# The first feed-forward rows handled inside the last attention turns

## The chip, the cores and the metric

The kernel runs on one core of one Trainium2 chip. The metric is the device time of one execution in microseconds (us); shorter is better. Where a profile is read, its own execution has a time and a span of its own, and both are named.

## The reference

A one-layer language model on 64 sequences of 128 tokens, model width 512. Everything is float32.

```
h = table[x] + lora_A.T[x] @ lora_B.T                       # embedding
h = h + attention(layernorm(h))                             # 16 heads, causal, low-rank q and kv
h = h + ffn(layernorm(h))

def ffn(x2):                                                # x2: 8192 x 512
    shared = x2 @ sw1.T * square(relu(x2 @ swg.T)) @ sw2.T  # hidden 256
    xl = x2 @ Wdown.T                                       # 128 wide
    probas = sigmoid(x2 @ Wg.T)                             # 16 experts
    top 8 of (probas + biases) per token; p = probas there, scaled to sum 2.5
    acc = sum over experts e of w[:, e] * (xl @ rw1[e].T * square(relu(xl @ rwg[e].T)) @ rw2[e].T)
    return shared + acc @ Wup.T
```

## The kernel before, in words

Each matrix product is made of three passes over a value split in a high and a low part (`split_matmul`): high times high, high times low, low times high. ScalarE (ACT) usually copies the high part out, VectorE (DVE) subtracts it to get the low part. "Splitting a piece" of the weights is such a pair of copies.

The program has two phases, each an engine-by-engine program of its own in a block. A block ends in a barrier that all engines must reach, and the next one starts behind it. Buffers in SBUF are allotted per phase, so nothing of the second phase is in place before the first one is over.

The **attention phase** treats 16 groups of 4 sequences (512 tokens) in a software pipeline. It is written out as turns n = -2 to 16 of 16 steps each. In turn n the scores, exponentials and head outputs of group n are made, while the front of group n+2 (`FRONT`: the gather's part `art`, the embedding rows `h`, the transposes `xt` of the normalised rows, the down projection `wd`) and the output projection `out` of group n-1 run between them. Tables (`MIDWAY`, `END`) say which of these parts stands in which step, and `has_part` says in which turns it exists: the front is absent in turns 14, 15 and 16, which have no group left to open. In turn 16 only the last head outputs of group 15 and its output projection are left. PE is TensorE. The SP queue issues all plain transfers in order: it stores the embedding rows `h`, loads them again into `res`, DVE adds the projection (`add_out`), and SP stores the result to the DRAM array `h2`. At its end SP waits for all these stores (`stored`).

The **expert phase** (`ffn_phase`) treats 16 groups of 512 rows of `h2`, group 0 by straight code, the rest in a loop. A group's front is: load `x`, statistics and inverse deviation on DVE, normalise on ACT, transposes on PE, high part `fxT_hi` and low part `fxT_lo`, the gate's product (`route_logits`), the down projection (`to_latent`), routing on DVE, and the two shared hidden halves. For groups 1 to 15 it is done between the expert products of the group before. For group 0 it stands alone at the phase's start, together with the constants (`gate`, identity) and the first 8 of 16 weight pieces of 128x1024, which come through staging buffers and are split on ACT and DVE. The routing weights leave as rows `wT` to the DRAM array `w_rows` and come back spread over all partitions (`w_all`, one transfer of 256 KB per expert); DVE multiplies by them in `weigh`. The remaining 8 pieces are loaded and split during group 0.

## Time and profile before

| | before |
|---|---|
| time, median of 3 runs (lowest, highest) | 2556.54 us (2556.44, 2558.4) |
| the profiled execution: its own time | 2557.69 us |
| the profiled execution: span | 2555.9 us |
| PE busy | 2434.7 us, 95% of the span |
| ACT busy | 1820.4 us, 71% |
| DVE busy | 1709.8 us, 67% |
| POOL (GpSimd) busy | 1131.6 us, 44% |
| mean granted TensorE clock | 0.987 of full |

The times of this document's traces are in microseconds from the start of the span. L401 is line 401 of the profiled kernel. Busy shares are means over the whole span; what one stretch waits for must be read in that stretch. The matmuls are pipelined, so the durations of two in a row overlap; what one costs is the distance of two starts.

### The profile page before, as it was taken

What the parts mean: (1) busy time and instruction counts of PE and PEld (TensorE: products, weight loads), DVE (VectorE), ACT (ScalarE), POOL (GpSimd) and SP (SyncE); (2) the same over time, 40 slices, a digit from 0 to 9 for tenths busy, and PEclk for the clock granted to TensorE, in tenths of its full rate; (3) what the DMA queues carried; (4) which work ended last, traced back from release to release, by engine and by line L of the source; (5) the groups of instructions that cost most, each with busy time, mean ns of one, the idle gap of its engine ahead of it and who ended that gap; (6) DMA issues with size and microseconds to landing.
All of it is one profiled execution on the core that took longest, in us unless ns stands there. A gap on an engine that the chain in (4) does not pass through costs nothing.

```text
span 2555.9 us, 47538 instructions
## 1 busy us (share of the span) xinstructions
PE 2434.7 (95%) x13632; PEld 1872.0 (73%) x13632; DVE 1709.8 (67%) x3614; ACT 1820.4 (71%) x4597; POOL 1131.6 (44%) x1275
## 2 busy tenths in 40 slices
PE   3899999999999996899999999999999999999999
PEld 2666666666777664678888888888888888878887
DVE  6777777777777763667567557657657657657655
ACT  2777777777777783677678668669668668668766
POOL 3444444444444331245445446436436445445444
PEclk8999999999999998899999999999999999999999
DMA  3222222222222112423213213212212221321321
GB/s 106 68 68 68 80 70 69 72 76 81 79 79 69 51 34 100 128 71 108 87 37 111 87 42 105 87 54 92 89 66 76 95 83 53 96 85 49 99 73 60
DMA packets 99830, 198.24 MB, mean 78 GB/s; under 512 B 10928, under 2 KB 10928, under 8 KB 99568
## 3 DMA queue, kind: packets, MB, share of 16 engines
q1 hardware_dynamic: 94576, 179.29, 21.2%
q0 software_dynamic: 5120, 17.31, 2.8%
q8 instruction: 67, 1.10, 0.2%
q14 instruction: 67, 0.55, 0.1%
HBM read 145.66 MB, written 50.86 MB: 77 GB/s over the span
## 4 chain that ended last, share of the span: by engine, by line
issue 30%; POOL 25%; PE 2%; DVE 1%; ACT 1%; POOLq 1%; DMA 0%; SPq 0%; DVEq 0%; ACTq 0%
POOL t_lo L1194 24%; POOL sh_lo L1194 2%; POOLq L1192 1%; DVE ps_u L1563 0%; DVE f_lo L1588 0%; ACT x L1357 0%; DMA x<-h 0%; DVE t L1570 0%; ACT t_hi L1412 0%; PE ps_g L1209 0%; PE fwork L1209 0%; PE ps_u L1211 0%; PE ps_u L1209 0%; PE ps_g L1211 0%; PE ps_g L1210 0%
## 5 line engine op out<-in xcount | busy, mean ns | idle before, releaser
L1194 POOL TENSOR_TENSOR t_lo<-t,t_hi 128x512 fp32r<-128x512 f32 x512 | 665.0, 1299 | 423.7 <-ACT t_hi L1412 423.6
L401 POOL TENSOR_TENSOR probs<-probs,inv 128x512 f32<-128x512 f32 x256 | 266.4, 1042 | 470.6 <-DVE inv L819 469.7
L1563 DVE TENSOR_TENSOR ps_u<-ps_u,square 128x512 f32<-128x512 f32 x512 | 357.2, 698 | 155.8 <-ACT square L1399 151.6
L1412 ACT ACTIVATE t_hi<-t 128x512 fp32r<-128x512 f32 x512 | 320.4, 626 | 121.0 <-PE ps_y L1211 68.3
L1570 DVE TENSOR_TENSOR t<-ps_u,w_all 128x512 f32<-128x512 f32 x512 | 354.1, 692 | 64.5 <-DVE ps_u L1563 22.4
L1395 ACT ACTIVATE square<-ps_g 128x512 f32<-128x512 f32 x544 | 319.7, 588 | 91.4 <-PE ps_g L1211 89.3
L637 ACT ACTIVATE probs<-ps_s,nmax 128x128 f32<-128x128 f32 x1024 | 364.1, 383 | 18.4 <-DVE nmax L813 17.3
L1399 ACT ACTIVATE square<-square 128x512 f32<-128x512 f32 x544 | 344.1, 633 | 17.3
L637 ACT ACTIVATION_READ_ACCUMULATOR probs<-ps_s,nmax 128x1 f32 x1024 | 228.7, 223 | 0.0
L1209 PE MATMUL ps_y<-t_hi,f_hi 128*128 128x512 f32 x512 | 210.2, 410 | 12.2 <-POOL t_lo L1194 12.0
L1194 POOL TENSOR_TENSOR sh_lo<-t,sh_hi 128x512 fp32r<-128x512 f32 x32 | 41.7, 1302 | 401.1 <-ACT sh_hi L1412 401.1
L1209 PE MATMUL ps_u<-xl_hi,f_hi 128*128 128x512 f32 x512 | 201.6, 394 | 5.3 <-DVE t L1570 5.3
L1209 PE MATMUL ps_g<-xl_hi,f_hi 128*128 128x512 f32 x512 | 201.1, 393 | 0.0
L1211 PE MATMUL ps_u<-xl_hi,f_lo 128*128 128x512 f32 x512 | 201.0, 393 | 0.0
L1210 PE MATMUL ps_y<-t_lo,f_hi 128*128 128x512 f32 x512 | 200.9, 392 | 0.0
L1211 PE MATMUL ps_y<-t_hi,f_lo 128*128 128x512 f32 x512 | 200.7, 392 | 0.0
L1211 PE MATMUL ps_g<-xl_hi,f_lo 128*128 128x512 f32 x512 | 200.6, 392 | 0.0
L1210 PE MATMUL ps_u<-xl_lo,f_hi 128*128 128x512 f32 x512 | 200.6, 392 | 0.0
L1210 PE MATMUL ps_g<-xl_lo,f_hi 128*128 128x512 f32 x512 | 200.3, 391 | 0.0
L644 ACT ACTIVATE pT<-ps_t 128x512 f32<-128x512 f32 x256 | 158.4, 619 | 29.7 <-PE ps_t L535 27.9
L813 DVE TENSOR_REDUCE nmax<-ps_s 128x8 f32<-128x1024 f32 x128 | 156.0, 1219 | 26.4 <-PE ps_s L526 25.7
L535 PE MATMUL ps_t<-ident,probs 128*128 128x128 f32 x1024 | 164.6, 283 | 9.2 <-ACT pT L644 7.7
(198 smaller groups left out, 5380.8 us busy)
## 6 DMA issues: line engine op xcount, KB each, us to landing
w_all<-w_rows SPq DMA_DIRECT2D x256, 256.0 KB, 3.2
h<-h SPq DMA_DIRECT2D x64, 256.0 KB, 2.1
res<-h SPq DMA_DIRECT2D x64, 256.0 KB, 2.8
h<-res SPq DMA_DIRECT2D x64, 256.0 KB, 2.0
x<-h SPq DMA_DIRECT2D x16, 1024.0 KB, 5.7
fres<-h SPq DMA_DIRECT2D x16, 1024.0 KB, 7.5
out<-fres SPq DMA_DIRECT2D x64, 256.0 KB, 2.1
fres<-in_w_ffn SPq DMA_DIRECT2D x14, 512.0 KB, 3.6
```

What stands on the lines that cost most here:

```text
L401: pool.tensor_tensor(probs[:, s % RING, :, :], probs[:, s % RING, :, :], inv[:, s % RING, :].rearrange("p (h o) -> p h o", o=1).to_broadca ...
L535: mm = pe.transpose(ps_t[:, j * P:(j + 1) * P], probs[:, s % RING, j, :], ident[:, :])
L637: e = act.activation(probs[:, s % RING, j, :], ps_s[:, b, x, i, y, :], ACT.Exp, bias=nmax[:, b, x, i, y:y + 1], accum_out=total[:, s % RIN ...
L1194: pool.tensor_tensor(lo, t[:, t_slot(j), :], hi.bitcast(F32), ALU.subtract).then_inc(t_lo_done, 1)
L1209: pe.matmul(o, a_hi, b_hi, start=first, stop=False)
L1210: pe.matmul(o, a_hi, b_lo, start=False, stop=False)
L1211: return pe.matmul(o, a_lo, b_hi, start=False, stop=last)
L1395: act.activation(square[:, j % 2, :], ps_g[:, j % 2, :], ACT.Relu).then_inc(relu_done, 1)
L1399: act.activation(square[:, j % 2, :], square[:, j % 2, :], ACT.Square).then_inc(square_done, 1)
L1412: act.activation(dst, t[:, t_slot(j), :], ACT.Copy).then_inc(t_hi_done, 1)
L1563: dve.tensor_tensor(dst, product, square[:, j % 2, :], ALU.mult).then_inc(t1_done, 1)
L1570: dve.tensor_tensor(t[:, t_slot(j), :], ps_u[:, u_bank(j), :], w_all[:, e % 2, :], ALU.mult).then_inc(t_done, 1)
```

## The change: what it does

- Buffers that both phases use are allotted once, outside both: the attention's `h` becomes `rows` (the experts' `x`), its `xn` becomes `keep` (the experts' staging and residual buffer), its `res` also holds `w_all` and `wT`, and `xT_hi`, `xT_lo`, the identity and the gate's buffers are shared.
- Turn 14 of the attention gets the part `xt` again, with statistics and normalisation, for a "group 16": the first 512 rows of `h2`, which turn 1 finished. SP loads them at the start of turn 14, with gate and biases; DVE prepares the gate.
- At the start of turn 15 SP loads weight pieces 0 to 3 into `keep` and `rows`.
- In turn 16 the output projection waits for each quarter (chunk) of the head outputs by itself, and for tiles 0 and 1 the first two of four chunks are issued in steps 0 and 1, ahead of the last head outputs.
- SP no longer waits for the last stores at the end of the attention; the experts wait for them where they reuse `res`.
- The experts' group 0 begins with `route_logits`. Pieces 4 to 7 are loaded after the barrier, pieces 8 and 9 after the first two spreads, group 1's rows ahead of the routing rows. Splits, routing and the shared halves stand in another order.

```diff
     if part == "out":
         return not any(is_turn(n, k) for k in (-2, -1, 0))
+    if part == "xt":
+        return not any(is_turn(n, k) for k in (GROUPS - 1, GROUPS))
...
         nw = sb("nw", [P, 5, 2 * TILES], F32)
-        xn = sb("xn", [P, TILES, D], F32)
-        xT_hi = sb("xT_hi", [P, DC, TOK], F32R)
-        xT_lo = sb("xT_lo", [P, DC, TOK], F32R)
+        xn, xT_hi, xT_lo = shared.keep, shared.xT_hi, shared.xT_lo
...
+            def load_first_rows():
+                sp.dma_start(shared.gate_raw[:, :, :], w_gate).then_inc(shared.small_loaded, 16)
+                sp.dma_start(shared.bias[:, :], biases).then_inc(shared.small_loaded, 16)
+                for t in range(TILES):
+                    wait_alone(sp, res_kept[t], 16 * GROUPS, sp_passed)
+                    wait_alone(sp, stored[t], 16, sp_passed)
+                wait_alone(sp, xn_done, TILES * GROUPS, sp_passed)
+                sp.dma_start(h[:, :, :], h2[0:TOK, :].rearrange("(t p) d -> p t d", p=P)).then_inc(rows_loaded, 16)
+
+            def load_first_pieces():
+                for t in (2, 3):
+                    bank, before = place(GROUPS - 2, "xt", t)
+                    wait_alone(sp, work_free[bank], DRAINS * (before + 1), sp_passed)
+                for i in range(4):
+                    sp.dma_start(piece_rows((shared.keep, shared.rows)[i // 2], i % 2),
+                                 w_ffn[:, i * PIECE:(i + 1) * PIECE]).then_inc(shared.piece_loaded[i], 16)
+
             def turn(n, side):
+                if is_turn(n, GROUPS - 2):
+                    load_first_rows()
+                if is_turn(n, GROUPS - 1):
+                    load_first_pieces()
...
-            for t in range(TILES):
-                sp.wait_ge(stored[t], 16 * GROUPS)
...
-                    if step == RSTD_AT and has_part(n, "h", 0):
+                    if step == RSTD_AT and has_part(n, "xt", 0):
...
-            def out_proj(n, side, t):
-                pe.wait_ge(oT_lo_done, DC * n)
-                for m in range(DC):
+            def out_proj(n, side, t, chunks=range(DC)):
+                if not is_turn(n, GROUPS):
+                    pe.wait_ge(oT_lo_done, DC * n)
+                for m in chunks:
+                    if is_turn(n, GROUPS):
+                        pe.wait_ge(oT_lo_done, DC * (n - 1) + m + 1)
...
+                        elif part == "out" and is_turn(n, GROUPS) and i < 2:
+                            mm = out_proj(n, side, i, range(2, DC))
...
+                    if is_turn(n, GROUPS) and step < 2:
+                        empty(pe, n, "out", step)
+                        out_proj(n, side, step, range(2))
...
-                drained(dve, n, "h", t)
+                if has_part(n, "h", t):
+                    drained(dve, n, "h", t)
+                else:
+                    dve.wait_ge(rows_loaded, 16)
...
-                front, rows = has_part(n, "h", 0), has_part(n, "ct", 0)
+                front, rows = has_part(n, "xt", 0), has_part(n, "ct", 0)
...
-                        if step == SPLIT_AT and not is_turn(n, GROUPS - 3):
+                        if step == SPLIT_AT and is_turn(n, GROUPS - 2):
+                            prepare_gate()
+                        elif step == SPLIT_AT and not is_turn(n, GROUPS - 3):
...
-FIRST_USES = 8
+FIRST_USES = 4
...
+        ident, gate, bias = shared.ident, shared.gate, shared.bias
+        x, res = shared.rows, shared.keep
...
+        w_all, wT = shared.res[:, 0:2, :], shared.res[0:EXPERTS, 2, :]
...
-            if i in (2, 3):
-                return (square, t)[i - 2][:, 0:2, :].rearrange("p b k -> p (b k)")
-            return res[:, :, :].rearrange("p t d -> p (t d)")[:, (i % 2) * PIECE:(i % 2 + 1) * PIECE]
+            if i in (4, 5):
+                return t[:, 2 * (i - 4):2 * (i - 3), :].rearrange("p b k -> p (b k)")
+            return piece_rows(x if i in (2, 3) else res, i % 2)
...
-                return 0
+                return -V_LOGITS // 2
...
-            sp.dma_start(gate_raw[:, :, :], w_gate).then_inc(small_loaded, 16)
-            sp.dma_start(bias[:, :], biases).then_inc(small_loaded, 16)
...
+                if before is None:
+                    wait_alone(sp, piece_lo, 4, sp_passed)
+                else:
...
-            load_x(0, None)
-            for i in range(EARLY_PIECES + 2):
+            for i in range(4, EARLY_PIECES):
                 load_piece(i)
+            load_x(1, None)
             store_rows(0)
+            for i in range(TILES):
+                wait_alone(sp, shared.stored[i], 16 * GROUPS, sp_passed)
             spread(0, 0)
             spread(0, 1)
+            for i in range(EARLY_PIECES, EARLY_PIECES + 2):
+                load_piece(i)
             def group(g, more):
-                if more:
+                first = isinstance(g, int) and g == 0
+                if more and not first:
                     load_x(g + 1, g)
-                first = isinstance(g, int) and g == 0
...
-            pool.memset(fident[:, :], 0.0).then_inc(f_ident, 1)
-            pool.wait_ge(f_ident, 1)
-            pool.affine_select(out=fident[:, :], in_=fident[:, :], compare_op=ALU.not_equal, fill=1.0,
-                               base=0, pattern=[[-1, P]], channel_multiplier=1).then_inc(f_ident, 1)
...
+                if isinstance(g, int) and g == 0:
+                    act.wait_ge(shared.stored[2], 16 * GROUPS)
                 full(act, half, k)
...
+            first = front_half(0)
             split(0)
-            for i in range(TILES):
-                normalise(0, i)
             split(1)
-            for i in range(TILES):
-                x_hi(0, 0, i)
+            logits_copy(0, first)
             split(2)
             split(3)
-            logits_copy(0, 0)
-            latent_hi(0, 0)
+            latent_hi(0, first)
+            logits_back(0, first)
+            sigmoid(0)
             split(4)
-            logits_back(0, 0)
-            sigmoid(0)
             split(5)
+            weights_copy(0, first)
             squares(0, 0)
             squares_end(0, 0)
             split(6)
+            hidden_hi(0, 0)
             squares(0, 1)
             squares_end(0, 1)
             split(7)
-            weights_copy(0, 0)
-            hidden_hi(0, 0)
             group(0, True)
...
-            dve.memset(gate[:, :, :].bitcast(F32), 0.0).then_inc(f_zeroed, 1)
-            dve.wait_ge(f_zeroed, 1)
-            dve.wait_ge(small_loaded, 32)
-            dve.tensor_copy(gate[:, :, 0:EXPERTS], gate_raw[:, :, :]).then_inc(small_step, 1)
-            dve.wait_ge(small_step, 1)
-            dve.tensor_tensor(gate[:, :, EXPERTS:2 * EXPERTS], gate_raw[:, :, :],
-                              gate[:, :, 0:EXPERTS].bitcast(F32), ALU.subtract).then_inc(small_step, 1)
-            for part in range(TILES + 1):
-                x_moments_of(0, part)
-            x_seed(0)
-            for k in range(3):
-                x_rstd(0, k)
-            x_shift(0)
-            split(0)
-            split(1)
-            for i in range(TILES):
-                x_lo(0, 0, i)
-            split(2)
-            split(3)
-            latent_lo(0, 0)
+            first = front_half(0)
+            for i in range(4):
+                split(i)
+            latent_lo(0, first)
+            routing(0, first)
             split(4)
-            routing(0, 0)
             split(5)
+            dve.wait_ge(piece_lo, 6)
             linear(0, 0)
             split(6)
             linear(0, 1)
```

Three places show how the instructions move. In these rows a bracket names the semaphores that an instruction waits for.

PE at the end of the attention (turn 16), before: `ps_t` are the transposes of the last probabilities, `ps_o` the head outputs, `work` with `oT_hi` the output projection.

```order
L535 MATMUL ps_t<-ident,probs 128x128 [waits pT_done,probs_done]
L535 MATMUL ps_t<-ident,probs 128x128 x3
L547 MATMUL ps_o<-pT,v 32x128 [waits pT_done,oT_lo_done]
...
L434 MATMUL work<-w_hi,oT_hi 128x512 [waits oT_lo_done,work_free0]
L435 MATMUL work<-w_lo,oT_hi 128x512
L436 MATMUL work<-w_hi,oT_lo 128x512
```

The same place now; the first row is the transposes of step 0.

```order
L591 MATMUL ps_t<-ident,probs 128x128 x3
L487 MATMUL work<-w_hi,oT_hi 128x512 [waits oT_lo_done,work_free0]
L488 MATMUL work<-w_lo,oT_hi 128x512
L489 MATMUL work<-w_hi,oT_lo 128x512
L487 MATMUL work<-w_hi,oT_hi 128x512 [waits oT_lo_done]
L488 MATMUL work<-w_lo,oT_hi 128x512
L489 MATMUL work<-w_hi,oT_lo 128x512
L591 MATMUL ps_t<-ident,probs 128x128 [waits pT_done,probs_done]
L591 MATMUL ps_t<-ident,probs 128x128 x3
```

Six projection matmuls of tile 0 stand between two sets of transposes; six of tile 1 stand behind the second set in the same way, so 12 of the 48 moved ahead of the head outputs.

DVE behind the barrier, before: `fstats` to `shift` are the first rows' statistics, `f_lo` a weight piece's low part, `fxT_lo` the transposed rows' low part, `xl_lo` the latent's.

```order
L1476 UNCONDITIONAL_BRANCH [waits barrier_Pool_Activation_PE_DVE_SP_release]
L1621 MEMSET gate 128x512
L1624 CAST gate<-gate_raw 128x4x16 [waits small_loaded,f_zeroed]
L1626 TENSOR_TENSOR gate<-gate_raw,gate 128x4x16 [waits small_step]
L1481 BN_STATS fstats<-x 128x6 [waits x_loaded] x4
...
L90 TENSOR_SCALAR shift<-fnw 128x4 [waits shift_done]
L1588 TENSOR_TENSOR f_lo<-fres,f_hi 128x1024 [waits piece_hi] x2
L1504 TENSOR_TENSOR fxT_lo<-fwork,fxT_hi 128x4x128 [waits fxT_hi_done] x4
L1588 TENSOR_TENSOR f_lo<-square,f_hi 128x1024 [waits piece_hi]
L1588 TENSOR_TENSOR f_lo<-t,f_hi 128x1024 [waits piece_hi]
L1511 TENSOR_TENSOR xl_lo<-fwork,xl_hi 128x512 [waits xl_hi_done]
```

DVE behind the barrier now:

```order
L1560 UNCONDITIONAL_BRANCH [waits barrier_Pool_Activation_PE_DVE_SP_release]
L1672 TENSOR_TENSOR f_lo<-keep,f_hi 128x1024 [waits piece_hi] x2
L1672 TENSOR_TENSOR f_lo<-rows,f_hi 128x1024 [waits piece_hi] x2
L1595 TENSOR_TENSOR xl_lo<-fwork,xl_hi 128x512 [waits xl_hi_done]
L1612 TENSOR_TENSOR route<-weights 128x64 [waits fwork_free0]
```

Gate, statistics and `fxT_lo` are gone from here; they stand in turn 14.

SP from turn 14 to turn 15 now; before, the rows of L376, L377, L382 and L389 did not exist. L407 is the store of a finished tile, L415 the reload of one.

```order
L415 DMA res<-h 128x512 [waits stored3,res_kept3]
L376 DMA gate_raw<-in_w_gate 128x64
L377 DMA bias<-in_biases 128x16
L382 DMA rows<-h 128x4x512 [waits res_kept0,stored0,res_kept1,stored1,res_kept2,stored2,res_kept3,stored3,xn_done]
L407 DMA h<-res 128x512 [waits work_free0]
...
L389 DMA keep<-in_w_ffn 128x1024 [waits work_free1,work_free0]
L389 DMA keep<-in_w_ffn 128x1024
L389 DMA rows<-in_w_ffn 128x1024 x2
L407 DMA h<-res 128x512 [waits work_free0]
```

The new loads stand between the last reload of one turn and the first store of the next.

## Rows read from the trace of the kernel before

**Rows 1.** Windows: busy us of PE, PEld, DVE, ACT, POOL; TensorE clock, DMA share, GB/s

```profile
860.20:916.80 56.60, 54.99 (x429) 39.36 (x429) 36.59 (x85) 44.91 (x170) 18.96 (x28) 1.00 0.12 39
916.80:965.20 48.40, 46.94 (x364) 31.90 (x366) 26.73 (x48) 41.32 (x164) 16.59 (x16) 1.00 0.14 45
1006.80:1032.30 25.50, 3.89 (x17) 3.17 (x17) 11.52 (x37) 8.07 (x12) 0.50 (x2) 0.57 0.50 177
1060.90:1103.00 42.10, 38.12 (x143) 28.07 (x144) 39.28 (x68) 35.31 (x58) 20.67 (x16) 0.92 0.48 150
```

**Rows 2.** Waits, 975 to 1070 us: who waited for whom, total us, times, longest

```profile
PE fwork L1223 <- ACT x L1357: 17.8, 1, 17.8
```

**Rows 3.** Timeline of the SP queue: start, length, line, transfer

```profile
880.86 0.34 SPq L360 DMA_DIRECT2D res<-h  x1
916.81 6.74 SPq L352 DMA_DIRECT2D h<-res  x2
998.55 8.70 SPq L352 DMA_DIRECT2D h<-res  x4
1053.71 0.35 SPq L1141 DMA_DIRECT2D w_rows<-wT  x1
1057.25 0.81 SPq L1149 DMA_DIRECT2D w_all<-w_rows  x2
```

**Rows 4.** Timeline of PE: a transposed tile in attention, then turn 16

```profile
815.79 0.60 PE L465 MATMUL work<-ident,xn 128*128 128x128 f32 x4
816.22 0.60 PE L535 MATMUL ps_t<-ident,probs 128*128 128x128 f32 x4
...
986.62 1.09 PE L535 MATMUL ps_t<-ident,probs 128*128 128x128 f32 x4 [1.25 <-ACT pT L644]
989.51 1.93 PE L547 MATMUL ps_o<-pT,v 128*32 128x128 f32 x32
992.98 0.76 PE L434 MATMUL work<-w_hi,oT_hi 128*128 128x512 f32 x1 [1.53 <-DVE oT_lo L824]
...
996.52 0.41 PE L436 MATMUL work<-w_hi,oT_lo 128*128 128x512 f32 x1
1005.59 0.40 PE L436 MATMUL work<-w_hi,oT_lo 128*128 128x512 f32 x1
```

**Rows 5.** Timeline around the barrier: POOL and DVE

```profile
1009.39 0.20 POOL L1186 MEMSET fident<- 128x128 f32 x1 [22.07 <-POOLq L187]
1009.57 0.48 DVE L1621 MEMSET gate<- 128x512 f32 x1 [2.75 <-SPq L187]
```

**Rows 6.** Timeline of PE in the experts' opening

```profile
1032.29 0.76 PE L1233 MATMUL fwork<-fxT_hi,gate 128*128 128x512 f32 x1 [1.61 <-DVE fxT_lo L1504]
1037.53 0.40 PE L1210 MATMUL fwork<-fxT_lo,f_hi 128*128 128x512 f32 x1
1061.62 0.79 PE L1209 MATMUL ps_u<-xl_hi,f_hi 128*128 128x512 f32 x1 [5.06 <-DVE t L1570]
```

**Rows 7.** Timeline of ACT in the opening

```profile
1041.30 1.28 ACT L1383 ACT_TABLE_LOAD   x1
1042.76 1.04 ACT L1420 ACTIVATE f_hi<-fres 128x1024 fp32r<-128x1024 f32 x1
1051.77 0.59 ACT L1388 ACTIVATE wT<-fwork 16x512 f32<-16x512 f32 x1 [0.24 <-PE fwork L1257]
```

**Rows 8.** Timeline of DVE in the opening

```profile
1045.61 0.22 DVE L1547 SCALAR_TENSOR_TENSOR weights<-route,wsum 128x64 f32<-128x64 f32 x1
1047.48 1.22 DVE L1588 TENSOR_TENSOR f_lo<-fres,f_hi 128x1024 fp32r<-128x1024 f32 x1
1060.87 0.69 DVE L1570 TENSOR_TENSOR t<-ps_u,w_all 128x512 f32<-128x512 f32 x1 [6.12 <-DMA w_all<-w_rows]
```

**Rows 9.** DMA issues of the page: queue, form, count, KB, median us to landing

```profile
h<-res SPq DMA_DIRECT2D x64, 256.0 KB, 2.0
t<-in_w_ffn SPq DMA_DIRECT2D x1, 512.0 KB, 8.8
```

More of the change, by code:

```diff
@@ L12 @@
 from contextlib import ExitStack
+from dataclasses import dataclass
 F32 = mybir.dt.float32
@@ L180, in place, with attention_phase, piece_rows, attention @@
     return k % 2, before + k // 2
-def attention_phase(nc, table, tok, lora_b, w_attn, ln, h2):
+@dataclass
+class Shared:
+    rows: object
+    keep: object
+    res: object
+    xT_hi: object
+    xT_lo: object
+    ident: object
+    gate_raw: object
+    gate: object
+    bias: object
+    piece_loaded: list
+    small_loaded: object
+    gate_zeroed: object
+    gate_step: object
+    stored: list
+operands_of_attention = []
+def attention_phase(nc, *operands):
+    operands_of_attention.append(operands)
+def piece_rows(buffer, i):
+    return buffer[:, :, :].rearrange("p t d -> p (t d)")[:, i * PIECE:(i + 1) * PIECE]
+def attention(nc, shared, w_ffn, w_gate, biases, table, tok, lora_b, w_attn, ln, h2):
     with ExitStack() as ctx:
@@ L195, in sem @@
             return ctx.enter_context(nc.semaphore(name))
-        ident = sb("ident", [P, P], F32)
+        ident = shared.ident
         ident_r = sb("ident_r", [P, P], F32R)
@@ L215, in attention_phase @@
         arT = sb("arT", [3 * RANK, TOK], F32R)
-        h = sb("h", [P, TILES, D], F32)
-        res = sb("res", [P, TILES, D], F32)
+        h, res = shared.rows, shared.res
         stats = sb("stats", [P, TILES, 6], F32)
@@ L289, in attention_phase @@
         res_loaded = [sem(f"res_loaded{t}") for t in range(TILES)]
-        stored = [sem(f"stored{t}") for t in range(TILES)]
+        stored = shared.stored
+        rows_loaded = sem("rows_loaded")
         dve_passed = sem("dve_passed")
@@ L957, in sb, with sem, experts @@
             return ctx.enter_context(nc.sbuf_tensor(name, shape, dt))
+        def sem(name):
+            return ctx.enter_context(nc.semaphore(name))
+        shared = Shared(
+            rows=sb("rows", [P, TILES, D], F32), keep=sb("keep", [P, TILES, D], F32),
+            res=sb("res", [P, TILES, D], F32), xT_hi=sb("xT_hi", [P, DC, TOK], F32R),
+            xT_lo=sb("xT_lo", [P, DC, TOK], F32R), ident=sb("ident", [P, P], F32),
+            gate_raw=sb("gate_raw", [P, DC, EXPERTS], F32), gate=sb("gate", [P, DC, P], F32R),
+            bias=sb("bias", [P, EXPERTS], F32), piece_loaded=[sem(f"piece{i}") for i in range(PIECES)],
+            small_loaded=sem("small_loaded"), gate_zeroed=sem("gate_zeroed"), gate_step=sem("gate_step"),
+            stored=[sem(f"stored{t}") for t in range(TILES)])
+        attention(nc, shared, w_ffn, w_gate, biases, *operands_of_attention.pop())
+        experts(nc, shared, h2, w_ffn, w_rows, out)
+def experts(nc, shared, h2, w_ffn, w_rows, out):
+    with ExitStack() as ctx:
+        def sb(name, shape, dt):
+            return ctx.enter_context(nc.sbuf_tensor(name, shape, dt))
         def pb(name, shape, dt):
@@ L976, in ffn_phase @@
         shift = sb("shift", [P, TILES], F32)
-        xT_hi = sb("fxT_hi", [P, DC, TOK], F32R)
-        xT_lo = sb("fxT_lo", [P, DC, TOK], F32R)
+        xT_hi, xT_lo = shared.xT_hi, shared.xT_lo
         xl_hi = sb("xl_hi", [P, TOK], F32R)
@@ L992, in ffn_phase @@
         weights = sb("weights", [P, TILES, 2 * EXPERTS], F32)
-        wT = sb("wT", [EXPERTS, TOK], F32)
-        w_all = sb("w_all", [P, 2, TOK], F32)
+        w_all, wT = shared.res[:, 0:2, :], shared.res[0:EXPERTS, 2, :]
         ps_g = pb("ps_g", [P, 2, TOK], F32)
@@ L999, in ffn_phase @@
         work = pb("fwork", [P, 2, 512], F32)
-        s_piece = [sem(f"piece{i}") for i in range(PIECES)]
+        s_piece = shared.piece_loaded
         piece_hi = sem("piece_hi")
         piece_lo = sem("piece_lo")
-        small_loaded = sem("small_loaded")
-        f_zeroed = sem("f_zeroed")
-        f_ident = sem("f_ident")
-        small_step = sem("small_step")
         x_loaded = sem("x_loaded")
@@ L1116, in load_x @@
             def load_x(g, before):
-                if before is not None:
+                if before is None:
+                    wait_alone(sp, piece_lo, 4, sp_passed)
+                else:
                     wait_drained(front_half(before), V_XT + 2)
@@ L1223, in x_turn @@
                     mm = pe.transpose(work[:, i % 2, m * P:(m + 1) * P], x[:, i, m * P:(m + 1) * P],
-                                      fident[:, :])
+                                      ident[:, :])
                 mm.then_inc(work_full[i % 2], 1)
             def route_logits(g, half):
-                drained(pe, half, V_XT + 2)
-                drained(pe, half, V_XT + 3)
+                if not (isinstance(g, int) and g == 0):
+                    drained(pe, half, V_XT + 2)
+                    drained(pe, half, V_XT + 3)
                 empty(pe, half, V_LOGITS)
@@ L1325, in group @@
                     logits_turn(g + 1, half)
-                    shared(g + 1, 0)
-                    shared(g + 1, 1)
+                    shared_half(g + 1, 0)
+                    shared_half(g + 1, 1)
                     weights_turn(g + 1, half)
```

71 lines of the change are left out of this document (36 added, 35 removed).

## The prediction

> **What bounds the kernel now.** I first read the busy shares over the span, which say that PE is the bound, and then asked in windows where it is not. In the attention's turns PE is busy nearly all the time: 54.99 of 56.60 us from step 8 of turn 13 to step 8 of turn 14, and 46.94 of 48.40 us one turn later [rows 1]. Between the phases it is not: from 1006.8 to 1032.3 us it does 3.89 us of work in 25.50 us [rows 1]. The waits name the cause: 17.8 us of PE waiting for ACT's normalised first rows [rows 2]. The timeline tells the rest. POOL leaves the barrier at 1009.39 us [rows 5]; call that R. PE's first product, the gate's, starts at 1032.29 [rows 6], that is R+22.9. Then the routing rows make their round trip through DRAM: `wT` is copied at 1051.77 [rows 7], stored by SP at 1053.71, spread from 1057.25 [rows 3], and DVE's first `weigh` starts at 1060.87 after 6.12 us of idleness [rows 8]. PE stands 5.06 us until 1061.62 [rows 6]. So the opening, from R to the first `weigh`, takes 51.5 us. Behind it DVE, with 39.28 of 42.10 us busy [rows 1], and not PE, limits group 0 while pieces 8 to 15 are split. So I measure the opening at DVE's first `weigh`.
>
> **Term 1, turn 14 (+1.9 us).** Four tiles of four transposes are added. PE takes 0.43 us from the start of such a tile to what follows it [rows 4], 4 x 0.43 = 1.7 us. PE is the bound there, so it is on the path; I add 0.2 for small waits. DVE gets the statistics, normalisation, four low parts and the gate, ACT four copies of high parts. DVE is busy 26.73 of 48.40 us in the later window and 36.59 in the earlier one [rows 1], so this has room and is costed at nothing; without that room it would show as waits of PE for `xT_lo`. Lower bound 1.7. Upper bound: the two windows differ by 56.60 - 48.40 = 8.2 us, which holds this work and the down projection too.
> The loads of turn 14 and 15 are put at nothing. SP issues nothing from 880.86+0.34 to 916.81 us [rows 3], and at about 882 all that they wait for is done; the four pieces go out at about 948, and the next store, of turn 15, is far off. Their price if late: turn 14's first stores would stand behind them.
>
> **Term 2, the attention's tail (-5.0 us).** Before, 48 projection matmuls run from 992.98 to 1005.99 [rows 4]. The clock is low at first (starts 0.43 us apart, full 0.23), and full from 996.52 on. Now 12 matmuls lie in the gaps where PE waits for ACT's copies, 1.25 us before 986.62 [rows 4]: six at full clock take 6 x 0.23 = 1.4 us. Three more (tile 0's third chunk) fill the 1.53 us wait for the last low part. 33 are left. At full clock they take 33 x 0.23 = 7.6 instead of 13.0 us, gain 5.4; with eight at the low clock, as before, 1.6 less, gain 3.8. If the denser work keeps the clock up, the head outputs of 1.93 us [rows 4] shrink by some 0.8 too, gain 6.2. Between 3.8 and 6.2 I take 5.0. Other bound: the six-matmul packets run at the low clock, 2.6 us each in gaps of 1.25; that delays the transposes behind them by 1.3 twice, gain 1.2.
> The Trainium skill ("TensorE: Matmul & The Clock Gate", Part 1 on the clock gate) says that PE is granted 2.4 GHz while it has been busy and 1.2 GHz after idleness. The trace agrees that the level falls in this sparse stretch. By that rule the packets would rather keep the clock up, gain 6.2 and a total 1.2 us lower than mine.
>
> **Term 3, no wait for the last stores (-1.7 us).** The last store is issued at 998.55+8.70 = 1007.25 us [rows 3]. Issued some 0.33 earlier, it lands 2.0 us later [rows 9], at about 1008.95; the barrier opens 0.45 later. Now it should open 0.45 after the issue, at 1007.7. Bounds: 0 (if the barrier itself takes that long) and 2.1.
>
> **Term 4, the opening (-29.6 us).** Gate, statistics, normalising, transposes and `fxT_lo` are gone from behind the barrier, and pieces 0 to 3 lie ready. From the new R on:
> - PE starts at R+0.2 at the low clock (it idled at the barrier): 8 gate matmuls x 0.43 = 3.4, to R+3.6. Before, the clock rose 5.2 us after 1032.29 (row at 1037.53 [rows 6]). So of the 12 down-projection matmuls four are slow: 1.7 + 8 x 0.23 = 3.5, to R+7.1.
> - ACT splits take 1.0 each [rows 7], DVE's 1.22 [rows 8]. Two splits, the logits copy at R+3.7, two more splits: piece 2 is done on DVE at R+6.5, piece 3 at R+7.7. PE's first shared half (24 matmuls x 0.23 = 5.6) goes from R+7.6 to R+13.2.
> - Routing: logits back at R+8.0, table load 1.28 [rows 7] to R+9.3; from a table load's end, 1042.58 [rows 7], to `weights`, 1045.83 [rows 8], it took 3.3: R+12.6. Weights turned behind the first half: R+13.7. `wT` copied, 0.59 [rows 7]: R+14.3. From 1053.71 to 1057.25 and on to 1060.87 the round trip takes 3.5 + 3.6 [rows 3, 8]: `w_all` is there at R+21.5. SP gets to the store at once, since its waits on pieces and rows ahead of it end by R+7.7.
> - Meanwhile PE's second half ends at R+19.3; DVE's product, split 7 and the next product (0.7 + 1.2 + 0.7) end at R+21.9. That is when `weigh` starts.
> 51.5 - 21.9 = 29.6. Bounds: PE at full clock throughout, 0.9 better; PE at the low clock through all 68 matmuls (0.2 us more for each of the 56 that I counted fast), 11 worse.
>
> **Term 5, behind it (-0.5 us).** PE's stretch of low clock after the 5.06 us wait disappears, worth 15 matmuls x 0.2 = 3.1, but DVE limits there. It waited only a little. From 0 to 3.1 I take 0.5. Pieces 8 and 9 are requested only after the spreads, at R+18 and R+21.2, and are used after R+25.
>
> **Sum.** 1.9 - 5.0 - 1.7 - 29.6 - 0.5 = -34.9 us. The profiled execution took 2557.69 us (span 2555.9); it becomes 2522.8. It lies 1.15 above the median of 2556.54, which becomes 2521.6.
>
> **The rivals.**
> - *The clock stays up* in turn 16 and early in the opening: 1.2 better there, 0.9 here and 1.5 of term 5: 2518. For it: the gaps are filled. Against it: PE must idle at the barrier. Chance 0.13, all gains beyond 2518 included.
> - *A transfer takes the place of the wait.* Pieces 4 and 5 go into `t` only behind the barrier; such a load took 8.8 us [rows 9] when many ran together, R+9.5, just when ACT wants it. Or piece 9, which waits on DVE's split 7, holds up SP's next spreads. Both have cover of 0 to 5 us. If it is used up, `weigh` slips by 3 to 7 us: 2525 to 2529. Chance 0.15.
> - *Code is late at the barrier.* Behind it each engine jumps to new code. Before, PE had 17.8 us of waiting to hide that [rows 2]; now nothing hides it. DVE began 0.2 us after POOL [rows 5], which speaks against it. The nearest row for a small transfer is the 3.5 us of the routing rows [rows 3]: with one or two on the path, 2525 to 2528. Chance 0.07. The Trainium skill ("Runtime: NRT & Kernel Launch", Instruction fetch mechanics) says that a taken branch to a page that is not at hand stalls until it is fetched. It names no price for it.
> - *The change doesn't do what it says*: the splits on ACT and DVE keep PE waiting as long as the rows did. They are 4 x 1.22 us in the stretch, so this would need each to wait for a transfer. Gain under 20, above 2537. Chance 0.04.
> - *Slower.* One mechanism: SP's queue. The load of the first rows waits in order for the last normalisation of turn 13; if it isn't free by 916.81, stores and reloads of turn 14 stand behind it and so does `add_out`. It has 35.6 us of room [rows 3], and must be late by that and 34.9 us more before the kernel is slower: over 2562. Chance 0.02, no change 0.01.
>
> **How the numbers follow.** The forecast, 2518.5 to 2525, has 0.58. With the clock rival and the two late ones a range of 2515 to 2529 holds what is wanted; bounds of term 1 and term 4 beyond it are left out with the last two rivals. About 0.2% (5 us) is what a measurement of this kernel tells from no change. Faster 0.97, same 0.01, slower 0.02.
>
> **What the changed profile would show.** Turn 14 about 2 us longer, without PE waits over 1 us for `xT_lo`. Last projection matmul 5 us earlier relative to the head outputs. Barrier under 1.2 us behind the last `add_out`. The gate's first matmul 0.2 us behind it, the first `weigh` 22 us behind it, with no PE wait of 5 us. Wrong it would be if PE, ACT or DVE stood several us right behind the barrier, if the store of `wT` came late on SP, or if the loss in turn 14 were above 4 us.

## The result, and the profile after

The changed kernel takes 2518.76 us (median; 2518.29 to 2520.05), the one before 2556.49 in the same comparison. The ratio is 0.9851, 95% interval [0.984, 0.9863]: 1.5% faster. The profiled execution took 2518.29 us, its span is 2516.5; that is 39.4 less than the span before. In what follows R is the first instruction behind the barrier: POOL at 1009.39 before [rows 5], SP at 1007.80 after.

The page of the changed kernel, and its windows (columns as in [rows 1]) over the part of turn 14 that got longer and over the opening:

```profile
span 2516.5 us, 47561 instructions
PE 2421.6 (96%) x13632; PEld 1866.1 (74%) x13632; DVE 1707.6 (68%) x3604; ACT 1814.8 (72%) x4593; POOL 1134.3 (45%) x1285
...
937.20:971.70 34.50, 32.19 (x255) 21.11 (x255) 20.18 (x38) 30.43 (x123) 11.39 (x11) 0.95 0.25 85
1006.10:1029.40 23.30, 21.32 (x95) 16.75 (x95) 16.49 (x34) 17.07 (x25) 3.12 (x2) 1.00 0.62 200
```

The second window is the gain. PE was busy for 3.89 of 25.50 us at the phase's start [rows 1]; now it is for 21.32 of 23.30, at full clock. The first shows what was paid: the clock is 0.95 where it was 1.00.

The SP queue, the counterpart of [rows 3]:

```profile
1000.12 7.30 SPq L407 DMA_DIRECT2D h<-res  x4
1007.80 0.84 SPq L1223 DMA_DIRECT2D t<-in_w_ffn  x2
...
1020.64 0.34 SPq L1228 DMA_DIRECT2D w_rows<-res  x1
1022.30 0.82 SPq L1236 DMA_DIRECT2D res<-w_rows  x2
```

The barrier opens 0.4 us after the last store is issued (1000.12 + 7.30 = 1007.42), no longer when it has landed. The routing rows are stored 12.8 us behind it, where it took 44.3, and spread 1.66 later (3.54 before).

PE in turn 16 and in the opening, the counterpart of [rows 4, 6]:

```profile
991.33 0.63 PE L591 MATMUL ps_t<-ident,probs 128*128 128x128 f32 x4 [1.16 <-ACT pT L705]
...
993.22 0.63 PE L591 MATMUL ps_t<-ident,probs 128*128 128x128 f32 x4
...
995.61 1.18 PE L603 MATMUL ps_o<-pT,v 128*32 128x128 f32 x32
998.24 0.50 PE L487 MATMUL work<-w_hi,oT_hi 128*128 128x512 f32 x1 [0.55 <-DVE oT_lo L888]
...
1005.78 0.39 PE L489 MATMUL work<-w_hi,oT_lo 128*128 128x512 f32 x1
1007.86 0.47 PE L1320 MATMUL fwork<-xT_hi,gate 128*128 128x512 f32 x1 [1.69 <-PEq L223]
```

The wait ahead of the second tile of `ps_t` is gone, since six matmuls fill it. The head outputs take 1.18 us instead of 1.93. The gate's first matmul starts 0.06 us behind R and is 0.47 us long instead of 0.76: full clock.

DVE and ACT up to the first `weigh`, the counterpart of [rows 7, 8]:

```profile
1018.39 0.23 DVE L1631 SCALAR_TENSOR_TENSOR weights<-route,wsum 128x64 f32<-128x64 f32 x1
1019.96 0.59 ACT L1475 ACTIVATE res<-fwork 16x512 f32<-16x512 f32 x1 [2.42 <-PE fwork L1344]
...
1027.50 0.70 DVE L1647 TENSOR_TENSOR ps_u<-ps_u,square 128x512 f32<-128x512 f32 x1
1028.23 0.69 DVE L1654 TENSOR_TENSOR t<-ps_u,res 128x512 f32<-128x512 f32 x1
```

`weigh` (`t<-ps_u,res`) follows the product ahead of it without a wait. It is no longer the round trip through DRAM that ends last there, but PE's shared halves and DVE's products.

### The profile page after: what moved, and what is told of

The parts are those of the page before. It is cut to its first block, busy times and chain, and to the rows that moved or that the text cites. A ratio compares the mean times of both kernels' runs of the same rounds, so it can differ in the third digit from the quotient of the medians.

```text
span 2516.5 us, 47561 instructions
## 1 busy us (share of the span) xinstructions
PE 2421.6 (96%) x13632; PEld 1866.1 (74%) x13632; DVE 1707.6 (68%) x3604; ACT 1814.8 (72%) x4593; POOL 1134.3 (45%) x1285
## 4 chain that ended last, share of the span: by engine, by line
issue 30%; POOL 26%; PE 2%; DVE 1%; ACT 1%; POOLq 1%; DVEq 0%; ACTq 0%
POOL t_lo L1280 24%; POOL sh_lo L1280 2%; POOLq L1278 1%; DVE ps_u L1647 0%; DVE f_lo L1672 0%; DVE t L1654 0%; ACT t_hi L1499 0%; PE fwork L1295 0%; PE ps_g L1295 0%; ACT square L1482 0%; PE ps_g L1297 0%; PE ps_g L1296 0%; PE ps_u L1297 0%; PE ps_u L1295 0%; PE ps_u L1296 0%
## 5 line engine op out<-in xcount | busy, mean ns | idle before, releaser
L1654 DVE TENSOR_TENSOR t<-ps_u,res 128x512 f32<-128x512 f32 x512 | 354.0, 691 | 55.5 <-DVE ps_u L1647 22.4
```

Source lines behind the costliest of these rows:

```text
L1654: dve.tensor_tensor(t[:, t_slot(j), :], ps_u[:, u_bank(j), :], w_all[:, e % 2, :], ALU.mult).then_inc(t_done, 1)
```

## The experiments

Each changes the changed kernel, except where said. Times of places come from the traces.

**Turn 16: the projection late again.**

```diff
-                        elif part == "out" and is_turn(n, GROUPS) and i < 2:
-                            mm = out_proj(n, side, i, range(2, DC))
...
-                    if is_turn(n, GROUPS) and step < 2:
-                        empty(pe, n, "out", step)
-                        out_proj(n, side, step, range(2))
```

> The changed kernel with one part undone: in turn 16 the output projection of all four tiles stands behind the last low part again, 48 matmuls in a row, as in the kernel before. Everything else is as changed. In the traces the stretch from the transposes of step 0 of turn 16 to the end of the last projection matmul took 21.25 us before and 14.84 us in the changed kernel. Theory 1 (15 matmuls moved into gaps, and with the gaps filled the clock stays at 2.4 GHz, so that the head outputs and the 33 left are fast too): this kernel takes some 21.2 us there, 6.4 more than the changed one, and its granted clock falls before the projection; time about 2525.1 us. Rival (only the matmuls moved count, 15 x 0.23 us, the clock stands high for another reason): 3.5 us more, 2522.2 us, with head outputs of 1.2 us and matmuls 0.23 us apart from the start.

2525.67 us, ratio 0.9878 [0.9861, 0.9894], thus 6.9 us slower than the changed kernel by the ratios, whose intervals just touch. But the profiled execution, the shortest of four, has a span of 2520.8, only 4.3 more, and a stretch of 19.14 us. So I took a second profile of this kernel:

> The same kernel as e_late_proj, profiled once more. Its profiled execution had a span of 2520.8 us and a mean granted clock of 0.995; its three other executions 2523.8 to 2525.8 at 0.993. Theory 1 (in these the clock fell in the thin stretch of turn 16 and stayed low into the 48 matmuls, as in the kernel before, where 13.01 us passed from the first of them to the end of the last): an execution with a span of 2523 to 2526 shows 12.5 to 13.5 us there, against 11.41 in the first profile. Rival (the low stretches are elsewhere, at the start of the kernel or in turn 14): a span of 2523 to 2526 with 11.4 us there and the first store of turn 1 later than 157. If the span is 2521 again, nothing is told.

The second span is 2523.6. PE's timeline in turn 16, first of the one execution, then of the other:

```profile
995.62 1.93 PE L600 MATMUL ps_o<-pT,v 128*32 128x128 f32 x32
999.09 0.47 PE L487 MATMUL work<-w_hi,oT_hi 128*128 128x512 f32 x1 [1.54 <-DVE oT_lo L880]
...
1010.10 0.40 PE L489 MATMUL work<-w_hi,oT_lo 128*128 128x512 f32 x1
```

```profile
991.08 0.63 PE L588 MATMUL ps_t<-ident,probs 128*128 128x128 f32 x4 [1.17 <-ACT pT L697]
...
995.19 1.94 PE L600 MATMUL ps_o<-pT,v 128*32 128x128 f32 x32
998.66 0.77 PE L487 MATMUL work<-w_hi,oT_hi 128*128 128x512 f32 x1 [1.53 <-DVE oT_lo L880]
...
1012.49 0.40 PE L489 MATMUL work<-w_hi,oT_lo 128*128 128x512 f32 x1
```

In both the head outputs run at 1.2 GHz (1.93 us). In the first the 48 matmuls start at full clock (0.47) and take 11.41 us, in the second at half (0.77) and take 14.23; the stretch is 21.81 us. One program, one place, 2.8 us apart by when the clock comes back; I had expected 12.5 to 13.5 us for the 48, so the half clock lasted longer than that. Theory 1 holds with 7.0 us in the second execution (14.84 to 21.81). In the first it is 4.3 us, with the clock low in the transposes and heads but not in the 48. The rival's 3.5 is only the part of the matmuls that were moved.

**Turn 16: one tile instead of two.** `i < 2` and `step < 2` above become `i < 1` and `step < 1`.

> The changed kernel with half of the early projection: in turn 16 only tile 0's first two chunks (6 matmuls) and its third stand in the gaps ahead; tile 1 is projected in one piece at the end as before. With all of it late the stretch from the transposes of step 0 of turn 16 to the end of the last projection matmul took 19.14 us, the eight head outputs in a row took 1.93 us (low clock), and the matmuls behind them stood 0.23 us apart; in the changed kernel it took 14.84 us and the head outputs 1.18. Theory 1 (one filled gap is enough to keep the clock): the head outputs take 1.2 us and the stretch is 6 x 0.233 = 1.4 us longer than in the changed kernel, 16.2 us. Rival (the clock falls in the second gap, which is empty again): the head outputs take 1.9 us and the stretch 17.0 to 18.5 us.

```profile
994.54 0.63 PE L591 MATMUL ps_t<-ident,probs 128*128 128x128 f32 x4
995.94 0.63 PE L591 MATMUL ps_t<-ident,probs 128*128 128x128 f32 x4 [0.78 <-ACT pT L705]
996.50 1.18 PE L603 MATMUL ps_o<-pT,v 128*32 128x128 f32 x32
```

The heads take 1.18 us although the second gap is open: in this execution one filled gap kept the clock. The stretch is 15.81 us (992.65 to 1008.46), 0.97 more than with two tiles, not 1.4: the second packet of six is longer than its gap and had put the heads off by 0.43 (from the first `ps_t` to the heads 3.85 here, 4.28 there). The time, 2521.58 us, ratio 0.9859 [0.9842, 0.9875], doesn't tell it from the changed kernel.

**The wait for the last stores, put back.**

```diff
             for n in range(-2, GROUPS + 1):
                 turn(n, n % 2)
+            for t in range(TILES):
+                sp.wait_ge(stored[t], 16 * GROUPS)
```

> The changed kernel with one part undone: SP waits again, at the end of the attention, for the last stores to land, so the barrier opens later. Theory 1: the opening keeps its length and only slides: from the end of the last add_out to the first issue behind the barrier 2.5 to 2.8 us instead of 0.8, and the whole time is 1.75 us longer, about 2520.5. Rival (the clock): PE idles 1.69 us at the barrier in the changed kernel and its first gate matmul still has the full clock; with 3.4 us of idleness the clock falls to 1.2 GHz, the first matmuls stand 0.43 us apart, and 8 to 20 of them at 0.2 us more put another 1.6 to 4 us on top: 2522 to 2524.

2522.7 us, 0.9866 [0.9849, 0.9882]; span 3.2 over the changed kernel's. The intervals of the two ratios overlap, so the reading rests on the trace. The opening in its timeline:

```profile
1009.55 0.76 PE L1320 MATMUL fwork<-xT_hi,gate 128*128 128x512 f32 x1 [3.46 <-PEq L223]
1010.11 0.63 PE L1320 MATMUL fwork<-xT_lo,gate 128*128 128x512 f32 x1
...
1015.22 0.39 PE L1297 MATMUL fwork<-xT_hi,f_lo 128*128 128x512 f32 x1
...
1031.98 0.69 DVE L1654 TENSOR_TENSOR t<-ps_u,res 128x512 f32<-128x512 f32 x1
```

The rival is right. The barrier is 1.8 us later (R at 1009.51), and behind 3.46 us of idleness PE runs at half clock until 1015.2: from R to `weigh` 22.47 us instead of 20.43. Dropping the wait is worth 1.8 us by itself and 2.0 by the clock up to `weigh`; 0.5 of it is made good again behind.

**The first weight pieces behind the barrier.** `load_first_pieces()` is not called; the experts' SP begins with `for i in range(EARLY_PIECES)` instead of `range(4, EARLY_PIECES)`.

> The changed kernel with one part undone: weight pieces 0 to 3 are not loaded in turn 15 but are SP's first issues behind the barrier, ahead of pieces 4 and 5. Theory 1 (the pieces' load is a part of its own of the gain): such a load took 8.8 us in the kernel before when several ran together, and 3.6 alone, so that the first split starts 4 to 7 us behind the barrier instead of at once. The gate's matmuls and the routing go on, but the down projection, the first shared half and all products behind it slip by that: the first product with square, 13.99 us behind the first issue in the changed kernel, comes at 18 to 21, and the time is 4 to 7 us longer, 2523 to 2526. PE idles there and falls to the low clock as well, which could put 1 to 3 us more on it. Rival (the round trip of the routing rows covers it): the weights of the experts were spread by 24 us behind the barrier at the latest, so up to 2 us of slip cost nothing, and the time is under 2 us longer.

```profile
1011.98 1.06 ACT L1505 ACTIVATE f_hi<-keep 128x1024 fp32r<-128x1024 f32 x1 [14.25 <-DMA keep<-in_w_ffn]
...
1014.35 0.80 PE L1293 MATMUL fwork<-xT_hi,f_hi 128*128 128x512 f32 x1 [4.17 <-DVE f_lo L1670]
```

The first split starts 3.9 us behind R (1008.07), PE stands 4.17 us and comes back at half clock. From R to `weigh` it takes 26.39 us, 5.96 more: the down projection starts 3.9 us later behind R, and its 12 matmuls take 4.77 us from first to last start instead of 2.67. The time is 2525.68 us, 0.9878 [0.9862, 0.9895]. Theory 1 holds; the round trip covers nothing.

**Turn 14: the inversion first.** The row in question, in the changed kernel's timeline of DVE, POOL, PE and ACT:

```profile
940.97 0.61 ACT L660 ACTIVATE xT_hi<-work 128x512 fp32r<-128x512 f32 x1
941.68 0.69 DVE L813 TENSOR_TENSOR xT_lo<-work,xT_hi 128x512 fp32r<-128x512 f32 x1 [2.13 <-ACT xT_hi L660]
942.29 0.17 DVE L883 RECIPROCAL inv<-total 128x4 f32<-128x4 f32 x1
942.53 1.04 POOL L454 TENSOR_TENSOR probs<-probs,inv 128x512 f32<-128x512 f32 x1 [3.04 <-DVE inv L883]
943.63 0.82 PE L591 MATMUL ps_t<-ident,probs 128*128 128x128 f32 x4 [1.96 <-POOL probs L454]
945.23 2.08 PE L582 MATMUL ps_s<-k_diag,qT 64*128 64x256 f32 x8
```

DVE stands 2.13 us at `xT_lo`, whose `xT_hi` is behind four exponentials on ACT. The reciprocal behind it has its totals already: with the edit below it runs before this wait. POOL and then PE wait for it, and the clock falls to half (2.08 us for what takes 1.14).

```diff
-                    if step in INVERT_FIRST and has_slot(n, step - INV_LAG):
+                    early = step in INVERT_FIRST or (is_turn(n, GROUPS - 2) and step == SPLIT_AT)
+                    if early and has_slot(n, step - INV_LAG):
```

> The changed kernel with one thing more: in turn 14 DVE inverts the totals of step 13 ahead of the other work of step 14, thus ahead of the low part of transposed tile 3, which waits for ACT. Theory 1 (head of the line): the low part of tile 3 blocks DVE's queue for 2.1 us, the reciprocal behind it is late, POOL's scaling of the probabilities behind that, and PE waits 1.96 us, upon which the clock falls to half for 3 us. With the reciprocal ahead the wait of PE is under 0.5 us, the clock stays up, and 2.5 to 3.1 us come back in turn 14: about 2515.5 us. Rival (it is POOL or ACT that is late in turn 14, by the added copies of xT_hi): the reciprocal comes earlier, PE's wait stays above 1.5 us and the time within 0.5 us of 2518.3. A third way: the gate's three operations behind it, 2.2 us in all, delay the next two reciprocals, so that a second wait appears and only 1 to 2 us come back.

```profile
939.41 0.18 DVE L883 RECIPROCAL inv<-total 128x4 f32<-128x4 f32 x1 [0.40 <-ACT probs L698]
942.85 0.69 DVE L813 TENSOR_TENSOR xT_lo<-work,xT_hi 128x512 fp32r<-128x512 f32 x1 [2.13 <-ACT xT_hi L660]
943.38 0.63 PE L591 MATMUL ps_t<-ident,probs 128*128 128x128 f32 x4 [1.08 <-ACT pT L705]
944.37 1.13 PE L582 MATMUL ps_s<-k_diag,qT 64*128 64x256 f32 x8
```

DVE waits as long as before, but nothing that is ready stands behind it. From turn 13's first store to turn 15's it takes 107.40 us instead of 109.81, the clock stays, and the time is 2516.65 us, 0.9841 [0.9825, 0.9857]. This interval overlaps that of the changed kernel, so the gain of the time is not shown by itself; that of the place is, since the changed kernel's profile and the five of the experiments above, which leave turn 14 alone, have 109.51 to 109.98 us there. A wait of 1.08 us is left, now for ACT.

**And the gate in turn 15.** `prepare_gate()` moves to step 8 of turn 15.

> The changed kernel with the inversion of turn 14 put ahead of the other work of step 14, as in the run before this one that did that alone, and with the gate's memset, cast and low part moved from DVE's step 14 of turn 14 to step 8 of turn 15. With the inversion alone, turn 14 was 2.4 us shorter (107.40 us from the first store of turn 13 to that of turn 15, against 109.81) and PE had one wait of 1.08 us left there, for ACT's pT. Theory 1: the gate's operations (1.25 us of DVE, and the gaps between them) still hold up the reciprocals of steps 14 and 15 in turn 14; with them gone another 0.3 to 0.7 us come back, about 2516. Rival: what is left is the four tiles of transposes themselves (1.75 us) and ACT's copy in front of pT, and the gate costs nothing: 107.4 us again and 2516.5.

From turn 13's first store to turn 15's it takes 107.38 us, and the time is 2517.71 us, 0.9848 [0.9832, 0.9865]: the rival's case; the gate costs nothing.

**Placement: the kernel before with the experts' buffers elsewhere.** The groups of the loop got shorter, and the attention's turns longer, without a changed instruction. In the kernel before `x`, `fres`, `w_all`, `wT`, 2 KB unused, `fxT_hi`, `fxT_lo`, `fident` and the gate's buffers are allotted ahead of `f_hi`.

> The kernel before, with nothing changed but the order in which the buffers of the feed-forward phase are allotted, so that every one of them (x, residual, w_all, wT, both halves of xT, the weights and all that follows) lies at the address that it has in the changed kernel. The attention's buffers stay where they were. The changed kernel took 93.49 us for a group of the feed-forward loop, the kernel before 93.83, with the same instructions. Theory 1 (the place of the buffers in SBUF sets how many nanoseconds a matmul takes): this kernel takes 93.5 us per group, 13 x 0.34 and a little at the ends, 5 to 6 us less in all: about 2551. Rival (it is something else that differs, such as where the instructions lie in memory, or one execution against another): 93.8 us per group and the time of the kernel before, within 1 us of 2556.5.

The first output store of groups 1 and 14, of before, of this kernel and of the changed one:

```profile
1249.47 0.36 SPq L1131 DMA_DIRECT2D out<-fres  x1
...
2469.32 0.36 SPq L1131 DMA_DIRECT2D out<-fres  x1
```

```profile
1247.76 1.47 SPq L1132 DMA_DIRECT2D out<-fres  x2
...
2463.48 5.55 SPq L1132 DMA_DIRECT2D out<-fres  x4
```

```profile
1215.62 5.51 SPq L1218 DMA_DIRECT2D out<-keep  x4
...
2430.89 5.53 SPq L1218 DMA_DIRECT2D out<-keep  x4
```

A thirteenth of the distance is 93.83, 93.52 and 93.48 us. (The profiles of the changed kernel and of its variants without pads lie between 93.48 and 93.56.) The place thus makes 4.1 of the 4.6 us that the 13 groups lost, and the median falls too: 2552.74 us, 0.9983 [0.9974, 0.9993]. Outside these groups it shows as well. From the first `weigh`, which here still waits for the round trip, to the end of the span it takes 1489.06 us instead of 1495.03:

```profile
1060.04 0.69 DVE L1571 TENSOR_TENSOR t<-ps_u,w_all 128x512 f32<-128x512 f32 x1 [6.06 <-DMA w_all<-w_rows]
```

The attention, whose buffers are not moved here, keeps its 58.59 us a turn (58.78 in the changed kernel; a twelfth of the distance from turn 1's to turn 13's first store).

**Placement: pads in the changed kernel.**

```diff
         ident = shared.ident
+        sb("pad", [P, 472], F32)
...
+        sb("fpad", [P, 152], F32)
         f_hi = sb("f_hi", [P, W_FFN], F32R)
```

> The changed kernel with two unused buffers and nothing else: 1888 bytes per partition ahead of the attention's own buffers, 608 ahead of the experts' own. The kernel before, with the experts' buffers placed as in the changed one, took 93.52 us per group of the loop instead of 93.83, so the place matters there. Theory 1 (what counts is how the two operands of a matmul lie to each other within 2 KB, or their alignment): the pad gives the attention's weights the distance from the transposed rows that they had in the kernel before, so that a turn takes 58.57 us again instead of 58.75; and it changes the groups' 93.49 by 0.1 us or more. Rival (what counts is in which region of SBUF a buffer lies, thousands of bytes away): 58.75 and 93.49 stay within 0.03.

58.56 us a turn, and 93.63 a group: both moved. The turn did so clearly (without a pad it is 58.77 to 58.81 in eight profiles), the group by 0.07 us beyond the range above. The median is 2517.13 us, 0.9844 [0.9827, 0.986]. The profiled execution, at 2521.29 us, was the longest of four; its start was late (first store of turn 1 at 159.97, not 156.53), with the down projections ahead of it at half clock for longer. With 32 bytes in either place (8 elements):

> The changed kernel with 32 unused bytes per partition ahead of the attention's own buffers and 32 ahead of the experts' own. This puts the attention's weights, which begin 32 bytes past a multiple of 64, onto a multiple of 64 like the transposed rows, and takes the experts' weights off one. Theory 1 (alignment to 64 bytes counts): a turn falls from 58.78 to about 58.56 us as with the pad of 1888 bytes, and a group gets longer than 93.50. Rival (the distance within some hundreds or thousands of bytes counts, which 32 bytes hardly change): 58.75 to 58.80 us a turn and 93.48 to 93.55 us a group.

58.69 us a turn and 93.60 a group, less than half of the way in the turns; 2518.56 us, 0.9847 [0.9832, 0.9862]. So alignment to 64 bytes is not the whole of it, and neither theory holds alone. Where it sits can be read from the mean distance between the starts of neighbouring matmuls, worked out from the timelines (48 of each over three turns; other turns give means up to 1 ns away). The first two rows are the down projection's 256-column matmuls, the third the output projection's of 512 columns:

```
                          before   after   pad 1888   pad 32
w_hi,xT_hi -> w_lo,xT_hi   131.9   137.1   130.4      135.4 ns
w_lo,xT_hi -> w_hi,xT_lo   115.2   119.4   114.8      118.3 ns
w_hi,oT_hi -> w_lo,oT_hi   255.0   255.8   255.6      256.0 ns
```

Those that read `xT`, which was moved relative to the attention's weights, change by 4 to 7 ns between before, the changed kernel and the pad of 1888 bytes; those that read `oT`, which was moved together with the weights, don't. Forty-eight such distances a turn at 4.2 ns make the 0.2 us.

**The gains together**: inversion first, gate in turn 15, the pad of 1888 bytes.

> Three things put together on the changed kernel: the inversion of turn 14 ahead of step 14's other work, the gate's preparation in turn 15, and an unused buffer of 1888 bytes per partition ahead of the attention's own buffers (none ahead of the experts'). Theory 1 (the gains add, because they come at different places): turn 13's first store to turn 15's 107.38 us less two turns' 0.22, so 106.9; 58.56 us per turn instead of 58.78, 16 x 0.22 = 3.5 us in all; groups of 93.5 us. The time is 2516.7 - 3.5 = about 2513 us (ratio to before about 0.983). Rival (the pad's gain in the turns is lost at the start of the kernel, where the padded kernel's first store was 3.4 us later than the others', 159.97 against 156.5): the turns are as short, the first store is at 159 to 160 us, and the time is within 1 us of 2516.7. If the later start was a matter of the clock in one execution, it is at 156 to 158 here.

2513.7 us (2512.57 to 2517.38), ratio 0.983 [0.9816, 0.9843], span 2511.9. It has turns of 58.59 us, groups of 93.52, 107.15 us in turns 13 and 14, first store at 156.95. I had expected 106.9 us for turns 13 and 14; of the two only turn 13 has a down projection, so the pad's 0.2 us comes once. The gains add, and the start is not late here, so that the late one was a matter of an execution. This is the fastest version here, about 5 us below the changed kernel by the ratios (0.983 against 0.9851), though the intervals still touch.

## Why the prediction was right, term by term

| term | predicted | in the traces |
|---|---|---|
| 1, turn 14 | +1.9 | +4.9 (104.95 to 109.81) |
| 2, tail | -5.0 | -6.4 (21.25 to 14.84) |
| 3, stores | -1.7 | -1.8 (2.57 to 0.81) |
| 4, opening | -29.6 | -31.1 (51.48 to 20.43) |
| 5, behind it | -0.5 | -6.8 (1495.0 to 1488.3) |
| turns up to 13 | 0 | +1.7 (860.22 to 861.93) |

They sum to -39.4, the difference of the spans; -34.9 was forecast. The time, 2518.8, lies in the range and below the 2521.6: a chain right in its kind, with terms 1 and 2 off in size, and one cause, the placement, that was not in it. That the errors partly cancelled is luck. So is that the time lies in the main forecast, 2518.5 to 2525: the clock rival, to which I gave 0.13, is what happened in turn 16 and in the opening.

- **Term 1 was mis-sized**, 4.9 instead of 1.9. The transposes came as costed (some 1.7). "So this has room and is costed at nothing" is the step that failed: DVE had room on average but not in order. A part that waits for ACT stood ahead of one that was ready. In turn 13 the low part of the same tile waits only 0.46 us, and PE has the down projection, which turn 14 lacks; that this is the cover I only argue. The inversion alone gave back 2.4. Some 1.5 of this is the clock: both padded kernels had PE's wait of 1.97 us there too, kept the clock, and from turn 14's first store to turn 15's took 51.48 and 51.43 us instead of 53.02. Of the signs that I had named, a loss above 4 us came; the wait of PE for `xT_lo` did not, it stood at the transposes, for POOL's `probs`.
- **Term 2** took the upper bound. The clock rival was right here: the 15 matmuls at 0.233 give 3.5, the heads 0.8, the slow ones among the 48 give 1.6 (13.01 us before, 11.41 at full clock), and the transposes ahead of the heads 0.9, less the 0.43 by which the second packet overruns its gap. The transposes' part was not in the working. In the two profiles of the undone kernel 0.8 and 3.5 us are left beyond the 3.5 of the 15 matmuls. The Trainium skill ("TensorE: Matmul & The Clock Gate", Part 1) says that the number of slow matmuls of one kernel differs from run to run, by the phase of the activity monitor. The two traces agree on the number: none of the 48 is slow in one, 14 are in the other. That the phase is the reason, no trace here shows.
- **Term 3** is right, but its edit is worth 3.8 us up to `weigh` (3.2 in the span) and not 1.8, since it keeps PE's idleness at the barrier to 1.69 us.
- **Term 4** assumed the low clock at R, "PE must idle at the barrier". With that clock (the store wait put back) the opening takes 22.5 us against the 21.9 of the sum, so the working was good to 0.6 us; the full clock gives 2.0, where I had put 0.9. The round trip was costed at 3.5 + 3.6 us; issue to issue it was 1.66 instead of 3.5, and it ended ahead of the products, so this cost nothing. The pieces laid ready are 6.0 us of the term: 3.9 for the wait and 2.1 for the low clock that follows it. No engine stood right behind the barrier for its code: PE starts 0.06 us and ACT 0.03 us behind SP. That rival falls. So does the transfer's: pieces 4 and 5 were split at 1015.55 without a wait.
- **Term 5** named a wait and missed what lay behind: 4.6 of its 6.8 us are 0.35 us in each of 13 groups. The placement run, with the wait of 5.05 us still in it, gives 6.0 of the 6.8 (1495.03 to 1489.06), so 0.8 is left for the wait that is gone, near the 0.5 that I had put. That the change re-allots all of SBUF stood in the diff. The placement costs the attention 0.19 us a turn, 2.3 up to turn 13; the first store was 0.6 earlier in this execution, which leaves the 1.7.

Open is what in an address makes a matmul some nanoseconds slower; the pads show only that 32 bytes as well as 1888 move it. Open is also why the clock stayed in turn 14 in both padded kernels and fell in all six profiles of the unpadded place; whether the pads do it, no run shows.

## What to carry to other kernels

Room on an in-order engine is not an average: where work is put into a turn, look at what is ready behind each of its waits. Short gaps of PE are worth filling beyond the matmuls that fit in them, and a wait ahead of a phase is worth dropping beyond its length, where the clock falls in them. After a change of allotment compare the loops that were not touched: a third of a microsecond in each of 13 groups was nearly as much as the whole of turn 14's loss (4.6 and 4.9 us).

## What the hardware showed that I had not expected

The same matmuls, in the same order, stand up to 7 ns further apart or closer by the place of their operands in SBUF; a loop group went from 93.83 to 93.52 us by this alone. PE was at full clock after 1.69 us of idleness at the barrier, at half after 3.46. After a like wait of PE in turn 14, 1.96 to 1.98 us, the changed kernel and its variants lost the clock in six profiles of six, and the two padded kernels kept it. The lines of the kernel with 1888 bytes, to be set beside those of the changed one (0.82 and 2.08 us):

```profile
944.30 0.66 PE L592 MATMUL ps_t<-ident,probs 128*128 128x128 f32 x4 [1.97 <-POOL probs L455]
...
945.32 1.13 PE L583 MATMUL ps_s<-k_diag,qT 64*128 64x256 f32 x8
```

The difference is some 1.5 us (53.02 against 51.48 us from turn 14's first store to turn 15's, where no matmul reads `xT`).
